# Masked graph attention over 6144 nodes: GpSimd makes h of the third tile behind tile 1's last flags instead of in front of v's first part

## What is computed

```
h      = maximum(layernorm(x), 0)
scores = einsum('md,de,ne->mn', h, weight, nodes)
scores = where(adj > 0, scores, -2**32 + 1)
out    = x + softmax(scores / 0.07, axis=1) @ nodes
```

## Time and profile before

| | |
|---|---|
| median of three executions | 930.68 us (929.98 to 930.69) |
| the profiled execution | 930.93 us |
| its span, first to last instruction | 929.2 us |
| TensorE (PE) busy | 912.7 us |
| VectorE (DVE) busy | 818.2 us |
| ScalarE (ACT) busy | 749.6 us |
| GpSimd (POOL) busy | 662.7 us |
| mean granted clock of TensorE | 0.998 of full |

### The profile page before, as it was taken

The page is one execution under the profiler, slowest core; times in us unless marked ns, Lnnn a source line. Parts: engine busy times, 40 slices in busy tenths (PEclk is TensorE's granted clock), DMA queues, the critical chain, the costliest instruction groups (busy, mean ns, idle before and its releaser), DMA issues.

```text
span 929.2 us, 25951 instructions
## 1 busy us (share of the span) xinstructions
PE 912.7 (98%) x7611; PEld 663.0 (71%) x7611; DVE 818.2 (88%) x1669; ACT 749.6 (81%) x1512; POOL 662.7 (71%) x450
## 2 busy tenths in 40 slices
PE   7989999999999999999999999999999999999997
PEld 4467777777777777777777777777777777777776
DVE  7889888998898889988998888888888888888985
ACT  6878878888888888888888888888888888888885
POOL 4999777677767776777677767776777677767712
PEclk9999999999999999999999999999999999999999
DMA  9799999999999999999999999999999999999955
GB/s 342 238 232 266 257 266 275 268 266 267 261 269 267 264 260 270 269 264 252 264 264 286 251 272 270 264 254 273 271 271 247 274 269 268 255 268 273 260 105 100
DMA packets 347401, 239.51 MB, mean 258 GB/s; under 512 B 308848, under 2 KB 327408, under 8 KB 328944
## 3 DMA queue, kind: packets, MB, share of 16 engines
q1 hardware_dynamic: 340176, 235.92, 99.2%
q10 hardware_dynamic: 7200, 3.28, 1.3%
HBM read 160.50 MB, written 3.15 MB: 176 GB/s over the span
## 4 chain that ended last, share of the span: by engine, by line
PE 91%; POOL 4%; DMA 2%; issue 1%; DVE 1%; SPq 1%; ACT 0%; POOLq 0%; DVEq 0%
PE ps_s L854 38%; PE ps_o L901 26%; PE ps_o L903 13%; PE ps_t L877 13%; POOL present L410 1%; POOL v L435 1%; DMA adj_i<-in_adj_dram 1%; POOL absent L419 1%; PE ps_s L847 1%; DMA pT_dma<-split 1%; POOL nodes_raw L432 0%; SPq L312 0%; DVE pT_lo L678 0%; DVE pT_hi L674 0%; SPq L338 0%
## 5 line engine op out<-in xcount | busy, mean ns | idle before, releaser
L655 DVE CUSTOM_DVE_ANT_0 probs<-ps_s,absent 128x1024 f32<-128x1024 f32 x288 | 351.7, 1221 | 48.2 <-PE ps_s L854 40.1
L419 POOL TENSOR_SCALAR absent<-present 128x2048 bf16<-128x2048 bf16 x142 | 296.3, 2087 | 64.2 <-DVE chunk_max L655 37.4
L410 POOL TENSOR_SCALAR present<-adj_i 128x2048 bf16<-128x2048 int32 x144 | 272.7, 1894 | 33.0 <-DMA adj_i<-in_adj_dram 27.1
L544 ACT ACTIVATE pT_hi<-ps_t 128x512 f16<-128x512 f32 x281 | 167.7, 597 | 157.2 <-PE ps_t L877 157.1
L901 PE MATMUL ps_o<-v,pT_dma 128*128 128x256 f16 x1152 | 220.9, 273 | 2.2 <-DMA pT_dma<-split 1.7
L514 ACT ACTIVATE ps_t<-probs,neg_max,exp_scale 128x512 f32<-128x512 f32 x285 | 220.3, 773 | 2.5 <-DVE neg_max L665 1.2
L678 DVE TENSOR_TENSOR pT_lo<-ps_t,pT_hi 128x512 f16<-128x512 f32 x284 | 194.7, 685 | 28.8 <-ACT pT_hi L544 28.1
L854 PE MATMUL ps_s<-yT_hi,hT_hi 128*128 128x512 f16 x576 | 218.6, 380 | 0.9 <-DVE chunk_max L655 0.9
L854 PE MATMUL ps_s<-yT_lo,hT_hi 128*128 128x512 f16 x576 | 218.7, 380 | 0.0
L901 PE MATMUL ps_o<-v,pT_hi 128*128 128x256 f16 x1152 | 206.3, 273 | 3.3 <-DVE v L722 2.6
L903 PE MATMUL ps_o<-v,pT_dma 128*128 128x128 f16 x1152 | 205.5, 219 | 0.0
(11 more groups left out here) (81 smaller groups left out, 610.0 us busy)
## 6 DMA issues: line engine op xcount, KB each, us to landing
adj_i<-in_adj_dram SPq DMA_DIRECT2D x144, 1024.0 KB, 5.3
pT_dma<-split SPq DMA_TRANSPOSE x288, 3.5
nodes_raw<-in_L_gnn_input_dram SPq DMA_DIRECT2D x6, 512.0 KB, 6.7
x_res<-in_x_dram SPq DMA_DIRECT2D x48, 64.0 KB, 4.9
out_dram<-fin ACTq DMA_DIRECT2D x48, 64.0 KB, 2.2
x_ln<-in_x_dram SPq DMA_DIRECT2D x46, 64.0 KB, 5.0
x_ln<-in_x_dram ACTq DMA_DIRECT2D x2, 64.0 KB, 3.2
w<-in_L_gnn_weight_dram SPq DMA_DIRECT2D x1, 64.0 KB, 2.1
```

Of the source, the lines that this page charges most:

```text
L410: nc.gpsimd.tensor_scalar(flags(s, c), adj_i[:, c, :], 1.0, 0.0, ALU.min, ALU.max)\
L419: nc.gpsimd.tensor_scalar(by_block(absent[:, c, :]), by_row(flags(s, c)), -ABSENT, ABSENT, ALU.mult, ALU.add).then_inc(absent_done, 1)
L544: nc.scalar.activation(pT_hi[:, p % BANKS, :], turn_area(k, at), ACT.Copy).then_inc(hi_done, 1)
L655: nc.vector.tensor_tensor_reduce(out=probs[:, s, j * SCORE:(j + 1) * SCORE], in0=ps_s[j % 2][:, :], in1=absent[:, c, part * SCORE:(part + ...
```

## The change

`make_h(2, 0, True)` is moved behind `v_lo_pool(0)`, `find_present(1, 1, 2)` and `make_absent(1, 1, 2, True)`. Nothing is added or taken away, and no wait is changed.

```
@@ -461,11 +461,11 @@
             find_present(1, 1, 1)
 
             make_absent(1, 1, 0, True)
-            make_h(2, 0, True)
             v_lo_pool(0)
             pool.wait_ge(absent_done, 4)
             find_present(1, 1, 2)
             make_absent(1, 1, 2, True)
+            make_h(2, 0, True)
 
             find_present(2, 0, 0)
             v_lo_pool(1)
```

## The result

Twenty executions each: 932.6 us with the change (930.26 to 934.75), 930.54 before (929.52 to 931.98). The ratio is 1.0019, with a 95% interval of 1.0013 to 1.0025: the change costs 1.8 us (0.0019 x 930.54; by the ends of the interval 1.2 to 2.3). The forecast was 932.3, that is +1.65. Two executions of later sets, one of each kernel (955.19 and 1360.76 us, at mean granted clocks of 0.947 and 0.656), ran in a slower state of the chip and are left out throughout.

A forecast was written before the change was run, and what follows sets the result against it. GpSimd was taken to bound the kernel until v's last low part near 61.1, TensorE from there; +0.03 (swap) +0.22 (L722's block) +1.4 (clock) = +1.65 us gave a median of 932.3, range 929.2 to 933.0.

The forecast's parts named there:

- What bounds the kernel: GpSimd leads until v's third low part ends at 61.07; product 9 waits for it, then TensorE works without a gap.
- Part 1: GpSimd's slot of h: v's first part and tile 1's last flags come 2.06 us earlier; the swap itself +0.03.
- Part 2: Readers of h, ready at 44.15 instead of 35.17: TensorE's turn has some 0.6 us to spare; cost 0.
- Part 3: SyncE's load of tile 2's last adjacency part goes at 40.9, 1.0 us earlier; taken as 0.
- Part 4: VectorE's mask of tile 1's scores 4 starts at 42.66, 1.81 us earlier; L722 wants to start at 44.41.
- Part 5: VectorE's L722 and GpSimd exclude each other, L722's own work 1.6 us; taken as +0.25, ends +1.67 and -1.35.
- Part 6: TensorE waits 3.6 us at product 9, 2.0 before product 3; a low clock at or just before 61.4 costs 1.4.
- The sum: Whole kernel: +0.03 (swap) +0.22 (L722's block) +1.4 (clock) = +1.65 us, median 932.3; chance 0.52.
- Rival A: TensorE's clock holds: no low clock granted, or it has passed before 61.4; 930.9 us, chance 0.22.
- Rival B: L722's 3.02 is its own work and holds up only L435; GpSimd gains 1.35, clock holds; 929.3, chance 0.12.
- Rival C: L722's 3.02 is its own work and blocks L410 throughout: GpSimd +1.67, clock falls, +1.7; 934.1, chance 0.08.
- Rival D: Some other wait keeps v's first part or L722 in place; L722 starts at 46.2; 930.7, chance 0.06.

The follow-up runs named there:

- first profile: A profiled execution of the changed kernel, no further edit, with no low clock recorded: 931.92 us.
- fills: Changed kernel with 14 extra matmuls in front of product 3 and 14 in front of product 9 of tile 0: 930.49 us, ratio 0.9998; again 930.05 us.
- second profile: Profile from running the changed kernel again with no edit; that set measured 932.29 us, ratio 1.0014.
- the probes: Kernel before with three extra two-input VectorE instructions of L722's kind, one where GpSimd is idle, two where it is not: one execution, 936.40 us.
- The fill at product 3: Changed kernel with 14 extra matmuls in front of product 3 of tile 0 only: 932.18 us, ratio 1.0020.
- a fill at product 9: Changed kernel with 14 extra matmuls in front of product 9 of tile 0 only: 931.6 us, ratio 1.0010; again 930.4 us, ratio 0.9999.

## Why the prediction was right, step by step

- **What bounds the kernel** (GpSimd to 61.1, TensorE from there): right. Every version that took work off GpSimd ahead of v's last part was faster; with h moved or a wait filled product 9 began between 60.7 and 61.6, whatever TensorE had done before.
- **Part 1**, the slot of h: right. 2.06 us was foreseen; v's first L435 began at 34.91 in the first profile, 1.99 earlier than in the earlier trace rows, and L410 of tile 2 at 44.22 and 44.05 (foreseen: 44.26). Counted from GpSimd's first flags, it came 0.04 and 0.11 us earlier than before, not 0.03 later (29.08 and 29.01 against 29.12).
- **Part 2**, h's readers: right, none waited. **Part 3**, SyncE's load: it went at 42.62 and 41.66, not at 40.9, since SyncE's transposes slipped with VectorE. It cost nothing.
- **Part 4**, VectorE: right in kind, wrong in how sure it was. The mask stopped waiting for flags, but began at 44.39 and 43.43, not at 42.66. I took "VectorE is free at 42.66" from one execution; it depends on TensorE's pace in the first 12 us, and the wait that the change removes had hidden that. In the five profiles of the changed kernel with fills and nothing else it began between 42.89 and 43.08.
- **Part 5**, L722 beside GpSimd: right. From the start of tile 2's L410 to the end of v's last part it took 16.83 us before and 16.98 in the second profile (61.03 - 44.05): +0.15, where I had +0.22. The alternatives at +1.67 and -1.35 did not occur. The instruction's own work was put at 1.6, and alone it takes 1.75; behind a wait it is 1.60 (45.94 to 47.54 here). The recorded text equates the 1.38 us that L435 was lengthened by with its overlap with L722, which is 1.52 (49.24 - 47.72); the difference is small and not explained.
- **Part 6**, the clock: right in place, and its price was set a little low. The wait at product 3 is 1.16, not 2.0, since TensorE came to it later itself; from there to product 9 it takes 10.12 us (47.60 to 57.72), foreseen 10.01. The wait at product 9 is 3.37 (foreseen 3.6), the low stretch follows 0.5 us behind its end, and it costs 1.7 (932.6 - 930.93), not 1.4, because nearly all of it falls behind the wait. The upper end of 932.7 for the forecast is 932.6 by its own terms.
- **The sum**: partly luck. GpSimd's two terms were put at +0.25. Counted from GpSimd's first flags, product 9 begins 46.05 us later in the second profile and 46.01 in the kernel before, so they came to +0.04: the +0.15 of the block is nearly made up by the earlier L410. The clock's term was 0.3 too small, GpSimd's 0.2 too large. Together 1.7; foreseen 1.65, measured 1.8.
- **Rival A** is what 4 executions of 20 did (930.93, forecast for it 930.9).
- **Rival B** falls with the probes (1.75 us alone). **Rival C** needed L722's 3.02 to be its own work and falls with them. **Rival D** is half true of the first profile: L722 was at 46.13 there, held by VectorE's late start, and its 931.92 instead of 930.7 goes with the wait of 1.3 for a transpose.

Four executions of 20 show 0.996 and 933.9 us, as if two low stretches counted. No profile of the changed kernel caught one. The fill at product 3 did not remove them (3 of 11), but none of the 44 executions of the changed kernel with a fill at product 9 has one, so they too hang on the wait there; where the second stretch lies remains open. A mean of 0.996 need not be two stretches: the probes' profile has it with a single one of 6.8 us, from 22.7 to 29.5, which begins while TensorE is idle for 5.23 us (19.87 to 25.10).

## What to carry to other kernels

A stall taken off an engine that is not the last to arrive only lengthens the wait at the next meeting point; look there before counting the gain. For TensorE the length of that wait matters, not only its end: 3.4 us in one piece brought, in most executions, a low clock that cost another 1.7, and 1.5 us of useless matmuls in it bought that back. Here a stretch of low clock that was followed by a wait for something else cost nothing (930.61 with it, 930.77 without), so moving the idle time from in front of that wait into it can cost 1.7 us though every engine does the same work.

## What the runs showed of the hardware

A lengthened instruction can be the mark of another engine. VectorE's instruction with two inputs in SBUF takes 1.75 us alone and is recorded with 2.36 to 4.72 when a GpSimd instruction is under way; GpSimd's, asked for meanwhile, are recorded with 3.06 instead of 1.53 (L432), 3.52 instead of 1.89, 4.49 instead of 3.11. The wait is inside the duration and shows in no list of waits. Even between two GpSimd instructions that follow back to back VectorE got its turn; where both began at the same moment (46.22), GpSimd went first and VectorE waited for all of its 3.10.

Unexpected was L792, a VectorE instruction with a single tensor of 128x128 in SBUF: 1.79 us instead of the 0.28 that it takes in the kernel before, where GpSimd is idle. It began at 15.11 and ended at 16.90, just behind GpSimd's L411 (16.81). The Trainium skill, page SBUF — State Buffer, section Who interferes with whom, names this case: a tensor_scalar may run in a mode that uses both ports, and then it too excludes GpSimd. The row agrees.

The granted clock of a stretch at the start of a kernel can read 1.00 while matmuls go at nearly half pace: two L920 in 1.91 us against 1.02. That the clock is the cause is an inference from the same pace at 0.50.
